# Six of the twelve copies that stack K, issued from ScalarE's queue in a sixteen-sequence transformer layer

## The reference

```
x = x + LN(attention(LN(x)))
x = x + LN(ffn(LN(x)))

attention: q = h Wq_down' Wq_up'        16 heads of 32
           c = h Wkv_down'              128 features
           k, v = c k_up, c v_up
           softmax(q k' / sqrt(32) - slope_h |i - j|, causal) v, then Wo'
ffn:       4-bit weights, dequantised by groups of 128
           y = (silu(gate) * up) W_down', divided by its root mean square
```

## Time and profile before

| | |
|---|---|
| median of three runs | 2572.87 us (2570.24 to 2573.47) |
| the profiled execution's own time | 2573.7 us |
| its span, first to last instruction | 2571.7 us |
| PE busy | 2440.2 us, 95% |
| DVE busy | 1524.9 us, 59% |
| ACT busy | 1468.6 us, 57% |
| GpSimd (POOL) busy | 671.7 us, 26% |
| mean granted clock of TensorE | 0.983 of full speed |
| DMA engines' mean share on the one queue in use | 15.9% |

### The profile page before, as it was taken

The page is one execution under the profiler, slowest core; times in us unless marked ns, Lnnn a source line. Parts: engine busy times, 40 slices in busy tenths (PEclk is TensorE's granted clock), DMA queues, the critical chain, the costliest instruction groups (busy, mean ns, idle before and its releaser), DMA issues.

```text
span 2571.7 us, 38700 instructions
## 1 busy us (share of the span) xinstructions
PE 2440.2 (95%) x13372; PEld 1112.6 (43%) x13372; DVE 1524.9 (59%) x4210; ACT 1468.6 (57%) x3935; POOL 671.7 (26%) x711
## 2 busy tenths in 40 slices
PE   5579999999999999999999999999999999999978
PEld 2334444444444444444444444444444444444433
DVE  3857566564756666475565646656574665657442
ACT  2756647465574746557474665747566474756610
POOL 0431322313232231322213132322313222131322
PEclk9699999999999999999999999999999999999989
DMA  3212120201212011121201112030121202012000
GB/s 110 45 34 50 34 66 18 66 18 50 50 34 66 18 51 34 50 50 34 66 18 44 41 42 58 26 74 18 36 48 42 58 23 74 14 42 50 22 12 17
DMA packets 99558, 109.65 MB, mean 43 GB/s; under 512 B 22885, under 2 KB 73189, under 8 KB 99301
## 3 DMA queue, kind: packets, MB, share of 16 engines
q1 hardware_dynamic: 99362, 107.19, 15.9%
HBM read 39.24 MB, written 16.78 MB: 22 GB/s over the span
## 4 chain that ended last, share of the span: by engine, by line
PE 77%; SPq 7%; DVE 6%; ACT 5%; DMA 2%; POOL 2%; issue 2%; POOLq 0%; DVEq 0%
PE dense L325 56%; PE psO L525 6%; SPq L1159 5%; PE score L509 4%; PE low L492 3%; PE psO L325 3%; PE score L492 3%; SPq L1209 2%; DMA kst<-arena 1%; DVE st_ln L762 1%; ACT arena L704 1%; PE low L509 1%; ACT low L630 1%; ACT L636 1%; DVE low L985 1%
## 5 line engine op out<-in xcount | busy, mean ns | idle before, releaser
L325 PE MATMUL dense<-arena,wgu 128*128 128x512 f16 x4224 | 1002.0, 379 | 11.2 <-DVE late L862 10.3
L325 PEld LDWEIGHTS dense<-arena,wgu 128*128 128x128 f16 x4224 | 405.9, 97 | 446.8 <-DVE late L862 17.6
L325 PE MATMUL dense<-wdn,arena 128*128 128x512 f16 x2112 | 533.0, 380 | 2.6 <-POOL arena L1076 2.6
L1076 POOL TENSOR_TENSOR arena<-late,arena 128x512 f16<-128x512 f32 x176 | 203.6, 1157 | 1046.2 <-DVE arena L883 1046.2
L985 DVE CUSTOM_DVE_ANT_0 low<-low,mmax 128x128 f32<-128x128 f32 (+3 forms) x672 | 278.1, 434 | 264.2 <-PE low L492 260.9
L704 ACT ACTIVATE arena<-score 128x512 f32<-128x512 f32 (+3 forms) x720 | 302.2, 440 | 188.3 <-PE score L509 145.2
L630 ACT ACTIVATE low<-low,ncol 128x128 f32<-128x128 f32 (+3 forms) x672 | 300.3, 447 | 140.8 <-DVE ncol L985 133.0
L630 ACT ACTIVATE score<-score,ncol 128x384 f32<-128x384 f32 x352 | 214.2, 609 | 165.7 <-DVE ncol L985 164.9
L325 PEld LDWEIGHTS dense<-wdn,arena 128*128 128x128 f16 x2112 | 199.2, 98 | 186.7 <-issue 11.5
L985 DVE CUSTOM_DVE_ANT_0 score<-score,mmax 128x384 f32<-128x384 f32 x352 | 214.6, 648 | 103.1 <-PE score L492 102.4
L1089 POOL TENSOR_SCALAR_AFFINE_SELECT arena<-arena 128x512 f32<-128x512 f32 x240 | 163.9, 683 | 278.7 <-ACT arena L704 276.4
(11 more groups left out here) (135 smaller groups left out, 2947.5 us busy)
## 6 DMA issues: line engine op xcount, KB each, us to landing
qst<-arena SPq DMA_DIRECT2D x384, 64.0 KB, 2.1
kst<-arena SPq DMA_DIRECT2D x192, 128.0 KB, 2.6
xin<-x SPq DMA_DIRECT2D x16, 1024.0 KB, 5.2
late<-x SPq DMA_DIRECT2D x64, 256.0 KB, 2.8
out<-late SPq DMA_DIRECT2D x64, 256.0 KB, 2.0
qst<-mrow SPq DMA_DIRECT2D x96, 8.0 KB, 1.9
wgu<-wo_t SPq DMA_DIRECT2D x1, 1024.0 KB, 44.9
wgu<-wq_down SPq DMA_DIRECT2D x1, 768.0 KB, 7.2
```

The costliest lines, as they stand in the source:

```text
L325: ins = nc.tensor.matmul(dst, w, a, start=first and k == 0, stop=last and k == len(tt) - 1)
L1076: nc.gpsimd.tensor_tensor(ht[:, 1, m, :], tb[:, m % 2, :], ht[:, 0, m, :], ALU.subtract).then_inc(sem["hl"], 1)
```

## The change

Between the high halves of Q2 and Q3, ACT now waits until the low half of K3 is written and then issues six of the twelve copies of K, those of heads 2 and 3 of each group of four (`a` = 2 and 3) in all three partition slots. SP issues the other six, where it issued twelve. Both count up the same semaphore, and what waits for it still waits for all twelve. This is so in all sixteen steps with attention.

```
--- before
+++ after
@@ -666,6 +666,14 @@
                     for g in range(2, NG):
                         high(job_q(t, g), qk[:, 0, g, :], HD ** -0.5 * S_QK / (S_X * S_WQ))
+                        if g == 2:
+
+                            taken(act, t, j["K"] + NG - 1)
+                            for slot, s in enumerate((0, 0, 1)):
+                                for a in range(2, HG):
+                                    nc.scalar.dma_start(
+                                        kst[HD * slot:HD * slot + HD, :, :].rearrange("p (g a) l -> p g a l", a=HG)[:, :, a, :],
+                                        qk[HD * a:HD * a + HD, 2 + s, :, :]).then_inc(sem["kstk"], 16)
                     if ffn:
 
                         act.wait_ge(sem["add2"], val("add2", t, 4))
@@ -1156,6 +1164,8 @@
                         for slot, s in enumerate(slots):
                             for a in range(HG):
+                                if done == "kstk" and a >= 2:
+                                    continue
                                 sp.dma_start(
```

## The result

The change makes the kernel slower: 2610.23 us (median of four runs, 2607.98 to 2612.52) against 2571.55 us. The ratio is 1.0151, with a 95% interval of 1.0133 to 1.0168, so +38.7 us. The direction is as predicted and the time lies in the range, but the forecast of 2591 us (+18.2 us) had less than half of the loss.

A forecast was written before the change was run, and what follows sets the result against it. PE was taken to bound the kernel, with its idle time as all that could be won. Longer gaps (+24.0 us) less the wait for K (-5.8 us) gave +18.2 us, so 2591 us; the range was 2568 to 2622 us.

The forecast's parts named there:

- The bound: PE bounds the kernel; SP's 5% of the chain is no price, only PE's idle time can be won.
- The wait for K: PE's wait for K's copies from SP's queue: it goes, -5.8 us, with 12.6 us as the other end.
- The wait on K3's low half: ACT's new wait before its copies: met 1.2 us before ACT comes to it, so it costs nothing.
- Six issues on ACT: Between the high halves of Q2 and Q3: 0.643 us each, 3.86 us in all, Q3 1.6 us late.
- the gaps: PE's waits at line 420 for DVE's normalising: 0.64 us grows to 2.2 us, +24.0 us over fifteen steps.
- The clock: PE's clock in the 2.2 us gap at line 420: no fall expected, the gap being well under 4 us.
- a rival with another cause: Whole issues of ACT and SP alternate: 2648 us, and a clock fall could add 52 us; chance 0.06.
- Step 0: ACT's 6.59 us wait for a weight covers the 1.6 us delay: nothing; without that cover 1.6 us.
- the first: Rival: ACT issues cheaply, at most 0.43 us each, only the wait for K goes: 2560 to 2567 us; chance 0.10.
- The second, queues in each other's way: Rival: each ACT copy waits for a piece of SP's issue, 0.343 us: 2622 us, chance 0.12.
- A third: Rival: shared DMA engines delay K's landing past 366 us, so K's wait stays: 2597 us; chance 0.02.
- What I said nothing gives back: The 1.6 us a step lost at line 420 isn't recovered later, since PE is busy nearly throughout.

The follow-up runs named there:

- the matmuls in the gap: The change plus nine needless 128x512 matmuls on PE before its wait for the third layer norm, steps 1 to 15: 2597.29 us, ratio 1.0106.

## Why the prediction was right, and where it was short

**The bound.** Right. The chain's 5% was no price, PE's own waits were. The wait for K went in every step. It was worth 8.0 us, between the two ends (5.8 and 12.6 us), so the row that I took was 2.2 us low. That the modelled end of a matmul hides part of such a wait is likely, but not shown.

**The wait on K3's low half.** Right, it costs nothing.

**Six issues on ACT.** The mechanism was right and its size a little under: 0.73 us from one copy to the next beside SP's, not 0.643 us. That ACT's sequencer issues on while the high half of Q2 runs is shown too (358.36 against 358.35 us). Q3 was 1.84 us late on average, where I took 1.6 us: the gaps cost 27.6 us instead of 24.0 us.

**The clock.** This is the step that failed: "in my forecast the gap of 2.2 us is well under the 4 us that the clock outlived", so the term was 0, and it measured 14.6 us. I had read one long wait in step 16 and taken the time until the clock fell there for what any gap may last. Behind gaps of 2.3 to 2.7 us it fell in ten of fifteen steps, and the matmuls in the gap took that term away. I had put the fall of the clock, at 3.5 us a step, into a rival with another cause; a fall cost 1.5 us.

**Step 0.** "I cost step 0 at nothing" was wrong. The cover that I named, ACT's wait for a weight, did hide ACT's delay; but the copies also ran beside SP's weight loads, which are on the path there. That is 3.2 us of the 5.3 us by which step 1 began late; the rest may be what step 0 differs by anyway.

**The sum.** 27.6 + 14.6 - 8.0 + 5.3 = 39.5 us, against the measured 39.1 us of span; predicted 24.0 + 0 - 5.8 + 0 = 18.2 us. That the time lay in the range was partly luck. My own forecast ended at 2600 us; the range went on to 2622 us for a piece of SP's issue waited out at each copy. The 2610 us came from the clock and step 0 instead.

**The rivals.** The balance point of the first, 0.50 us an issue for six copies or 2.98 us in all, is borne out by four copies: 2.6 to 3.1 us in the steps of their trace, and no difference in time. The second, queues in each other's way, holds in a mild form only: 0.09 us a copy, not 0.34. A third: K landed later (3.5 us instead of 2.6), and nothing waited.

**What I said nothing gives back** wasn't given back: the gaps' growth stands whole in the account.

## What to carry to other kernels

Before a queue's issues are moved to an engine that computes, take the time that this engine has between the two instructions around the new place, divide by what one issue costs, and move only so many; here three and a half, and 4 us were won with three where six lost 39. Follow the next instruction behind them to whoever waits for it: the same six copies cost 38.7 us or gave 7 us, by one instruction's place on VectorE. And when two waits of the bounding engine lie one behind the other, removing the earlier one alone can move its time into the later one: it brought nothing here (1 us, within the noise). The later one has to go as well, and both together brought 18 us, where the later one alone brought 4 us.

## What the runs showed of the hardware

- The granted clock fell to 0.50 just after PE resumed behind gaps of 2.31 to 2.68 us in ten of fifteen steps of the change, behind 2.12 to 2.81 us in nine of fifteen of the change without copies in step 0, and behind 2.68 us in eight of fifteen with eight needless activations. It stayed there 3.4 us each time. At line 420 it fell in no step with a gap of up to 1.73 us (three, four and five copies, six needless activations, the matmuls in the gap). In step 16 it had fallen during the wait itself.
- The gap's length alone doesn't decide: of the fifteen equal gaps of 2.68 us, eight were followed by a fall and seven weren't. What decides between them stays open.
- DMA issues on ACT cost 0.630 us each and overlap the activation started just before them. ACT's queue issued six in 3.98 us while SP's was in one issue of 30.03 us.
- The copies from the second queue lengthened that one issue by 3.2 us for six, 0.5 us each, and by 0.3 to 0.4 us each for three to five.
